# Differential attention with an expert network: the value product of a block as one burst, the second exponentials scaled on GpSimd, the output evicted on VectorE, the out-projection moved up one step

## The chip, the core and the metric

The kernel runs on one core of a Trainium2 chip. The core has TensorE (matrix products, in the profile PE, its weight loads PEld), VectorE (DVE), ScalarE (ACT), GpSimd (POOL) and SyncE (SP), which issues nearly all transfers. The metric is the device time of one execution in microseconds (us); the median of three runs is given.

## What is computed

The reference normalises X (2 x 1024 tokens of 128 values), runs a differential attention with 16 heads on it, and an expert network of a main and two chosen experts per batch, and adds both to X. The attention, cut to what matters:

```python
A1 = jnp.einsum('bhqd,bhkd->bhqk', Q1, K1) * s
A2 = jnp.einsum('bhqd,bhkd->bhqk', Q2, K2) * s
P = jax.nn.softmax(A1, axis=-1) - lam * jax.nn.softmax(A2, axis=-1)
O = jnp.einsum('bhqk,bhkd->bhqd', P, V)
Ocat = jnp.transpose(O, (0, 2, 1, 3)).reshape(O.shape[0], O.shape[2], -1)
Y = Ocat @ Wo + bo
```

All is float32. The kernel writes the two softmaxes with their sums l1 and l2 of exponentials e1 and e2: it builds p = e1 - e2 * (lam * l1 / l2), multiplies by V and Wo, and puts the factor 1 / l1 on at the very end, when the rows are added to Y.

## The kernel before

The attention has 2 batches x 16 heads x 8 query tiles of 128 rows, 256 steps. Each engine has its own program, written out by hand, with counters (semaphores) between them; the order inside an engine is the order of its program. A function `step(g, k)` per engine gives what it does at one step; `attention` writes 16 steps (`BODY`, two heads) out, loops over them, and writes the first and last 16 out apart, with some steps behind the end in which the pipeline drains. Four steps make a block (`QB`), `kb` is the block and `j` the step in it.

One step, for query tile n, in the order in which its data flows:

- TensorE, `scores` (L502): two tiles of 128 x 1024 scores, s = 0 and 1, four instructions each, into one of three PSUM slots of 1024 columns. The slots go round over the score tiles and the projections of the next head.
- VectorE, `row_max` (L861): the maximum of each tile. ScalarE, `exps` (L683): the exponentials, s = 0 to `p_mix`, s = 1 to `e2_buf` (a part of `work`), both four steps deep, with their sums in `l_sum`.
- VectorE, one step later: reciprocals of both sums (L894) into `l_inv`, -lam * l1 (L895) into `l1_neg`, and the scaling of e2 with both factors, one TENSOR_SCALAR of 128 x 1024 (L899). It raises `scaled`.
- GpSimd: the addition e1 + e2 (L412), 128 x 1024, raises `mix_done`. The program of GpSimd also splits the weights of a head to come (`split_w`, L350 to L357, once in 8 steps), in the first steps prepares the expert network (L373 to L399), and in the last head splits its first weights (L426, L429).
- TensorE, `turn`, three steps later (`LAG`): eight transposes of p in two halves of four (L514), each half evicted by ScalarE (`evac_pt`, L696) to `pt`, which holds two blocks.
- TensorE, `pv` (L528): per block eight products of 128 x 64 weights (V) with 512 columns, even ones to the lower and odd ones to the upper 64 rows of the bank `o_ps`. They go in pairs; `PV_AT` puts pair 0 at the first half of step 3, pair 1 at its second half, and pairs 2 and 3 at the two halves of step 0 of the next block.
- ScalarE at step 1 evicts `o_ps` to `o_t` (L703, waits for `pv_done`). TensorE at step 2, first half, does the out-projection of four 128 x 128 products (`out_proj`, L540) into `o_ps` again. VectorE at step 2 adds the four tiles to `y_acc` with the factor 1 / l1 (`add_y`, L873) and raises `y_evac`, on which the next block's first pair waits.

Twice per head TensorE also does a projection of the next head (L458), of which ScalarE makes the high part (L662) and VectorE the low part (L806). Behind the attention comes the expert network (L585, L598, L732 to L738, L438, L958, L964).

On ScalarE the exponential of s = 0 waits until the transposes of the tile four steps back have been made, that of s = 1 until its addition has been made (both buffers are four deep). On TensorE the transposes of step n - 3 wait for `mix_done` and stand between the two score tiles of step n.

## Time and profile before

| | before |
|---|---|
| median of 3 runs | 1380.82 us (1380.06 to 1381.09) |
| profiled execution, whole time | 1380.4 us |
| its span | 1378.6 us |
| TensorE busy | 1292.9 us, 94% |
| VectorE busy | 1173.6 us, 85% |
| ScalarE busy | 1063.3 us, 77% |
| GpSimd busy | 783.6 us, 57% |
| mean granted TensorE clock | 0.99 |

The busy time of an engine counts its compute instructions. Matrix products are pipelined and their ends are modelled, so the shares of TensorE say less than the pitch from one group to the next. The profile's waits say how long an engine stood before a line and whose instruction ended that. An engine that isn't the bottleneck may stand idle at no cost, so the wait that ends last in a stretch is what matters.

### The profile page before, as it was taken

What the parts mean: (1) busy time and instruction counts of PE and PEld (TensorE: products, weight loads), DVE (VectorE), ACT (ScalarE), POOL (GpSimd) and SP (SyncE); (2) the same over time, 40 slices, a digit from 0 to 9 for tenths busy, and PEclk for the clock granted to TensorE, in tenths of its full rate; (3) what the DMA queues carried; (4) which work ended last, traced back from release to release, by engine and by line L of the source; (5) the groups of instructions that cost most, each with busy time, mean ns of one, the idle gap of its engine ahead of it and who ended that gap; (6) DMA issues with size and microseconds to landing.
All of it is one profiled execution on the core that took longest, in us unless ns stands there. A gap on an engine that the chain in (4) does not pass through costs nothing.

```text
span 1378.6 us, 21990 instructions
## 1 busy us (share of the span) xinstructions
PE 1292.9 (94%) x6658; PEld 859.8 (62%) x6658; DVE 1173.6 (85%) x1745; ACT 1063.3 (77%) x1787; POOL 783.6 (57%) x423
## 2 busy tenths in 40 slices
PE   3879999999999999999999999999999999998787
PEld 2646666666666666666666666666666666655576
DVE  7768888888888888888888888888888888886998
ACT  2168888888888888888888888888888888887764
POOL 3078555556555555555555565556555555576765
PEclk9999999999999999999999999999999999999988
DMA  6974444334333444444443343334444444400000
GB/s 146 331 165 103 102 102 102 87 86 92 86 85 87 98 103 103 103 103 102 99 103 89 85 92 87 85 87 95 103 103 103 103 103 99 99 1 1 1 16 16
DMA packets 89822, 129.37 MB, mean 94 GB/s; under 512 B 44484, under 2 KB 62404, under 8 KB 89796
## 3 DMA queue, kind: packets, MB, share of 16 engines
q1 hardware_dynamic: 89092, 128.89, 40.7%
q8 instruction: 14, 0.23, 0.1%
q10 hardware_dynamic: 576, 0.15, 0.1%
q14 instruction: 12, 0.10, 0.0%
q0 software_dynamic: 128, 0.01, 0.0%
HBM read 18.91 MB, written 9.44 MB: 21 GB/s over the span
## 4 chain that ended last, share of the span: by engine, by line
PE 62%; DVE 17%; issue 8%; ACT 5%; POOL 3%; SPq 3%; DMA 1%; DVEq 1%; ACTq 0%; POOLq 0%
PE ps L502 25%; PE ps L528 16%; PE ps L514 12%; PE ps L458 7%; DVE small L861 6%; DVE y_acc L873 3%; ACT pt L696 2%; PE ps L540 2%; DVE pt L964 2%; SPq L251 2%; POOL p_mix L412 2%; ACT p_mix L683 2%; DVE work L958 2%; DVE y_acc L943 1%; DVE work L806 1%
## 5 line engine op out<-in xcount | busy, mean ns | idle before, releaser
L412 POOL TENSOR_TENSOR p_mix<-p_mix,work 128x1024 f32<-128x1024 f32 x256 | 609.3, 2380 | 506.6 <-DVE work L899 506.6
L861 DVE TENSOR_REDUCE small<-ps 128x1 f32<-128x1024 f32 x512 | 619.8, 1220 | 161.6 <-PE ps L502 152.9
L502 PE MATMUL ps<-k_hi,q_st 128*128 128x512 f32 x1024 | 362.6, 435 | 8.1 <-DMA q_st<-work 4.3
L683 ACT ACTIVATE p_mix<-ps,small 128x1024 f32<-128x1024 f32 x256 | 286.8, 1120 | 103.8 <-DVE small L861 103.8
L696 ACT ACTIVATE pt<-ps 128x512 f32<-128x512 f32 x512 | 305.2, 596 | 66.4 <-PE ps L514 61.0
L683 ACT ACTIVATE work<-ps,small 128x1024 f32<-128x1024 f32 x256 | 286.3, 1118 | 70.0 <-DVE small L861 69.7
L514 PE MATMUL ps<-ident,p_mix 128*128 128x128 f32 x2048 | 311.2, 274 | 23.1 <-ACT pt L696 14.6
L502 PE MATMUL ps<-k_lo,q_st 128*128 128x512 f32 x1024 | 320.8, 395 | 0.0
L514 PEld LDWEIGHTS ps<-ident,p_mix 128*128 128x128 f32 x2048 | 241.7, 140 | 123.1 <-issue 38.7
L502 PEld LDWEIGHTS ps<-k_hi,q_st 128*128 128x128 f32 x1024 | 158.7, 189 | 195.9 <-issue 125.8
L528 PE MATMUL ps<-pt,v_h 128*64 128x512 f32 x1024 | 276.6, 619 | 0.0
L899 DVE TENSOR_SCALAR work<-work,small 128x1024 f32<-128x1024 f32 x256 | 227.9, 890 | 9.3
L502 PEld LDWEIGHTS ps<-k_lo,q_st 128*128 128x128 f32 x1024 | 192.4, 188 | 43.8
L438 POOL TENSOR_TENSOR work<-work 128x1024 f32<-128x1024 f32 x24 | 76.0, 3166 | 37.0 <-DVE work L958 37.0
L806 DVE SCALAR_TENSOR_TENSOR work<-ps,small,work 128x1024 fp32r<-128x1024 f32 x64 | 81.6, 1276 | 3.6 <-ACT work L662 3.5
L873 DVE SCALAR_TENSOR_TENSOR y_acc<-ps,small,y_acc 128x128 f32 (+1 forms) x256 | 71.8, 343 | 8.5 <-PE ps L540 7.8
L528 PEld LDWEIGHTS ps<-pt,v_h 128*64 128x64 f32 x1024 | 50.9, 135 | 44.4 <-issue 44.4
L662 ACT ACTIVATE work<-ps,small 128x1024 fp32r<-128x1024 f32 x64 | 71.7, 1120 | 8.2 <-PE ps L458 5.2
L598 PE MATMUL ps<-w,pt 128*128 128x128 f32 x384 | 55.1, 305 | 23.8 <-DVE pt L964 18.8
L598 PEld LDWEIGHTS ps<-w,pt 128*128 128x128 f32 x384 | 51.6, 216 | 31.3 <-DVE pt L964 23.7
L540 PE MATMUL ps<-wo_dup,o_t 128*128 (+1 forms) x512 | 67.7, 275 | 0.2 <-ACT o_t L703 0.2
L540 PEld LDWEIGHTS ps<-wo_dup,o_t 128*128 128x128 f32 x512 | 62.2, 192 | 0.6 <-ACT o_t L703 0.6
(118 smaller groups left out, 910.0 us busy)
## 6 DMA issues: line engine op xcount, KB each, us to landing
k_hi<-work SPq DMA_DIRECT2D x128, 256.0 KB, 4.8
k_lo<-work SPq DMA_DIRECT2D x128, 256.0 KB, 4.8
q_st<-work SPq DMA_DIRECT2D x128, 256.0 KB, 4.4
v_scratch<-pt SPq DMA_DIRECT2D x16, 512.0 KB, 6.4
v_h<-v_scratch SPq DMA_DIRECT2D x32, 256.0 KB, 4.4
wqk_raw<-in_L_attn_Wk SPq DMA_DIRECT2D x31, 64.0 KB, 1.7
wqk_raw<-in_L_attn_Wq SPq DMA_DIRECT2D x31, 64.0 KB, 1.9
x_all<-in_L_attn_X SPq DMA_DIRECT2D x2, 512.0 KB, 5.3
```

The lines of the kernel that those rows point to most:

```text
L412: pool.tensor_tensor(e1, e1, e2, ALU.add).then_inc(mix_done, 1)
L458: mm = pe.matmul(into[:, half * BANK:(half + 1) * BANK], wt[:, w * P:(w + 1) * P], a[:, bass.ds(t0 + half * BANK, BANK)], start=j == 0, st ...
L502: mm = pe.matmul(slot[SLOT[tile]][:, cols], qs4[:, par, s, q0:q0 + P], kk[:, par, s, cols], start=j == 0, stop=j == 1)
L514: mm = pe.transpose(pt_ps[:, c * P:(c + 1) * P], p_mix[:, col:col + P], ident[:, :])
L528: mm = pe.matmul(o_ps[half * D:(half + 1) * D, :], vh4[:, (kb // 2) % 2, c, :], pt4[:, kb % 2, c, :], start=c < 2, stop=c >= KC - 2, skip_ ...
L540: mm = pe.matmul(o_ps[:, t * E:(t + 1) * E], o_t[:, col:col + P], wo_dup[:, bass.ds(head * E, E)], start=True, stop=True, skip_group_check ...
L598: mm = pe.matmul(out_ps, hidden[u % 4][:, t * P:(t + 1) * P], w24[:, 0 if f == 0 else TOPK * b + f, c, :], start=i == 0 and t % 4 == 0, st ...
L683: act.activation((p_mix, e2_buf)[s][:, k % 4 * S:(k % 4 + 1) * S], slot[SLOT[k, s]], ACT.Exp, bias=neg_max[:, m:m + 1], scale=1.0, accum_o ...
L696: act.activation(pt4[:, kb % 2, half * 4:half * 4 + 4, j * P:(j + 1) * P], pt_ps.rearrange("p (c q) -> p c q", c=4), ACT.Copy).then_inc(pt ...
L861: dve.tensor_reduce(neg_max[:, m:m + 1], slot[SLOT[k, s]], AX.X, ALU.max, negate=True)\
L873: add = dve.scalar_tensor_tensor(out=tile, in0=o_ps[:, t * E:(t + 1) * E], scalar=l_inv[:, r1:r1 + 1], in1=tile, op0=ALU.mult, op1=ALU.add)
L899: dve.tensor_scalar(e2, e2, l_inv[:, r + 1:r + 2], l1_neg[:, e:e + 1], ALU.mult, ALU.mult)\
```

## The change

- The four pairs of a block's value product are issued in one piece, at step 3, first half, of the next block.
- The scaling of e2 goes from VectorE to GpSimd, ahead of the addition, as one TENSOR_SCALAR of 128 x 1024 with the same two factors. GpSimd now waits for the reciprocals (`recip_done`), and its addition waits for its own scaling (`scaled`). `l1_neg` becomes four columns deep, and VectorE waits, before it writes it, for the scaling of four steps before.
- The eviction of `o_ps` goes from ScalarE at step 1 to VectorE at step 0, behind the first maximum.
- The out-projection goes from step 2, first half, to step 0, second half, of the block; the sum into `y_acc` goes from step 2 to the end of step 1.
- On VectorE the reciprocals stand ahead of the second maximum of a step.
- GpSimd's steps are written out, with no loop.

```diff
-PV_AT = {(3, 0): 0, (3, 1): 2, (0, 0): 4, (0, 1): 6}
-OUT_AT = (2, 0)
+PV_AT = (3, 0)
+OUT_AT = (0, 1)
...
-        l1_neg = small[:, 172:174]
+        l1_neg = small[:, 172:176]
...
             def step(g, k):
-                n = g * BODY + k
+                n, km = g * BODY + k, (k - 1) % BODY
                 if now(g, k, 1):
-                    e1 = p_mix[:, (k - 1) % 4 * S:((k - 1) % 4 + 1) * S]
-                    e2 = e2_buf[:, (k - 1) % 4 * S:((k - 1) % 4 + 1) * S]
+                    e1 = p_mix[:, km % 4 * S:(km % 4 + 1) * S]
+                    e2 = e2_buf[:, km % 4 * S:(km % 4 + 1) * S]
+                    pool.wait_ge(recip_done, 2 * n)
+                    pool.tensor_scalar(e2, e2, l_inv[:, 2 * km + 1:2 * km + 2], l1_neg[:, km % 4:km % 4 + 1],
+                                       ALU.mult, ALU.mult).then_inc(scaled, 1)
                     pool.wait_ge(scaled, n)
                     pool.tensor_tensor(e1, e1, e2, ALU.add).then_inc(mix_done, 1)
...
-            attention(pool, step, 1)
+            for n in range(STEPS + 1):
+                step(n // BODY, n % BODY)
...
-            def pv(g, kb, c0):
+            def pv(g, kb):
...
-                for c in (c0, c0 + 1):
+                for c in range(KC):
...
-                back = 1 if j == 3 else 2
-                if (j, half) in PV_AT and now(g, k - j, back * QB):
-                    pv(g, kb - back, PV_AT[j, half])
+                if (j, half) == PV_AT and now(g, k - j, QB):
+                    pv(g, kb - 1)
...
-                if j == 1 and now(g, k - j, 2 * QB):
-                    act.wait_ge(pv_done, g * (BODY // QB) + kb - 1)
-                    act.activation(o_t[:, (kb % 2) * BANK:(kb % 2 + 1) * BANK], o_ps, ACT.Copy).then_inc(o_evac, 1)
...
                 if now(g, k):
                     row_max(g, k, 0)
+                if j == 0 and now(g, k - j, 2 * QB):
+                    dve.wait_ge(pv_done, g * (BODY // QB) + kb - 1)
+                    dve.tensor_copy(o_t[:, (kb % 2) * BANK:(kb % 2 + 1) * BANK], o_ps).then_inc(o_evac, 1)
...
-                if j == 2 and now(g, k - j, 2 * QB):
-                    add_y(g, kb)
-                if now(g, k):
-                    row_max(g, k, 1)
                 if now(g, k, 1):
                     dve.wait_ge(exp_done, 2 * m + 2)
+                    after(dve, scaled, m - 3)
                     dve.reciprocal(l_inv[:, r:r + 2], l_sum[:, l:l + 2]).then_inc(recip_done, 1)
                     dve.tensor_scalar(l1_neg[:, e:e + 1], l_sum[:, l:l + 1], lam_neg, None, ALU.mult)\
                         .then_inc(recip_done, 1)
-                    dve.wait_ge(recip_done, 2 * m + 2)
-                    e2 = e2_buf[:, km % 4 * S:(km % 4 + 1) * S]
-                    dve.tensor_scalar(e2, e2, l_inv[:, r + 1:r + 2], l1_neg[:, e:e + 1], ALU.mult, ALU.mult)\
-                        .then_inc(scaled, 1)
+                if now(g, k):
+                    row_max(g, k, 1)
+                if j == 1 and now(g, k - j, 2 * QB):
+                    add_y(g, kb)
```

## Rows read from the trace of the kernel before

**Rows 1.** The page's part 1: busy us, share of the span, instructions.

```profile
PE 1292.9 (94%) x6658; PEld 859.8 (62%) x6658; DVE 1173.6 (85%) x1745; ACT 1063.3 (77%) x1787; POOL 783.6 (57%) x423
```

**Rows 2.** Waits: engine, line, whom it waited for, us in total, times, longest.

```profile
POOL p_mix L412 <- DVE work L899: 506.6, 245, 18.6
```

**Rows 3.** Busy time of one head: PE, PEld, DVE, ACT, POOL, clock, DMA, GB/s.

```profile
680.70:717.70 37.00, 36.47 (x190) 23.74 (x188) 31.83 (x51) 30.51 (x53) 20.72 (x11) 1.00 0.43 95
```

**Rows 4.** The chain in order of time: start us, us it accounts for, what.

```profile
714.27 1.01 PE ps L528 x4
715.28 1.12 PE ps L502 x4
...
722.74 0.89 PE ps L540 x8
...
736.24 0.44 PE ps L514 x4
736.67 0.93 PE ps L502 x4
...
738.04 1.39 PE ps L458 x6
...
1259.74 1.87 PE ps L528 x8
```

**Rows 5.** Groups by form, VectorE and ScalarE: busy us, mean ns, idle before.

```profile
L861 DVE TENSOR_REDUCE small<-ps 128x1 f32<-128x1024 f32 x512 | 619.8, 1220 | 161.6 <-PE ps L502 152.9
L899 DVE TENSOR_SCALAR work<-work,small 128x1024 f32<-128x1024 f32 x256 | 227.9, 890 | 9.3
L806 DVE SCALAR_TENSOR_TENSOR work<-ps,small,work 128x1024 fp32r<-128x1024 f32 x64 | 81.6, 1276 | 3.6 <-ACT work L662 3.5
...
L703 ACT ACTIVATE o_t<-ps 128x512 f32<-128x512 f32 x64 | 37.6, 587 | 0.4 <-PE ps L528 0.4
```

**Rows 6.** GpSimd's groups by form, and line L399 alone (ns min/median/max).

```profile
L381 POOL TENSOR_SCALAR b_bc<-b_bc,small 128x128 f32<-128x128 f32 x5 | 2.9, 604 | 0.0
...
L363 POOL COPY y_acc<-gb_bc 128x2048 f32<-128x2048 f32 x1 | 1.9, 1887 | 0.0
...
L343 POOL CAST k_hi<-w_raw 128x1024 fp32r<-128x1024 f32 x1 | 1.0, 1041 | 5.8 <-DMA w_raw<-in_L_attn_Wv 5.8
...
L399 POOL TENSOR_SCALAR w<-w,small x5: 1560/1692/1952, 113.0 to 133.7; 128x512 f32<-128x512 f32 x5
```

**Rows 7.** Lines L412 and L899 alone: ns min/median/max, first and last start.

```profile
L412 POOL TENSOR_TENSOR p_mix<-p_mix,work x256: 2352/2378/2404, 67.4 to 1253.6; 128x1024 f32<-128x1024 f32 x128
...
L899 DVE TENSOR_SCALAR work<-work,small x256: 811/814/2766, 66.5 to 1250.7; 128x1024 f32<-128x1024 f32 x128
```

**Rows 8.** GpSimd in order of time: start us, us, line, operation, idle before.

```profile
166.61 2.39 POOL L412 TENSOR_TENSOR p_mix<-p_mix,work 128x1024 f32<-128x1024 f32 x1 [1.56 <-DVE work L899]
168.95 0.40 POOL L350 TENSOR_TENSOR wqk_raw<-wqk_raw,small 128x128 f32<-128x128 f32 x1
169.44 0.61 POOL L354 TENSOR_TENSOR wqk_hi<-wqk_raw,small 128x256 fp32r<-128x256 f32 x1
170.13 0.73 POOL L357 TENSOR_TENSOR wqk_lo<-wqk_raw,wqk_hi 128x256 fp32r<-128x256 f32 x1
```

**Rows 9.** Three steps of the last head, and TensorE in them.

```profile
1232.27:1247.59 15.32, 12.96 (x69) 8.77 (x70) 13.02 (x20) 12.14 (x21) 15.08 (x10) 1.00 0.00 0
...
1244.88 0.66 PE L514 MATMUL ps<-ident,p_mix 128*128 128x128 f32 x4 [1.30 <-POOL p_mix L412]
```

**Rows 10.** Busy time where GpSimd prepares the experts, and splits w1.

```profile
91.01:135.20 44.19, 38.41 (x188) 24.98 (x188) 31.46 (x49) 29.85 (x51) 39.57 (x34) 0.92 0.46 98
1224.22:1247.59 23.37, 20.97 (x109) 12.98 (x107) 20.99 (x30) 17.99 (x33) 22.35 (x15) 1.00 0.00 0
```

**Rows 11.** TensorE behind a transfer, and the granted clock of that stretch.

```profile
95.39 1.22 PE L502 MATMUL ps<-k_hi,q_st 128*128 128x512 f32 x2 [4.31 <-DMA q_st<-work]
...
95.00:100.00 5.00, 4.61 (x12) 2.33 (x12) 1.23 (x1) 1.65 (x3) 4.76 (x7) 0.50 0.03 7
```

More of the change, by code:

```diff
@@ L515, in turn @@
                 mm.then_inc(pt_ready, 1)
-            def pv(g, kb, c0):
+            def pv(g, kb):
                 blk = g * (BODY // QB) + kb
-                if c0 == 0:
-                    pe.wait_ge(pt_evac, 2 * QB * (blk + 1))
-                    after(pe, y_evac, blk)
-                    if kb % 2 == 0:
-                        pe.wait_ge(v_loaded[kb // 2], 16 * (g + 1))
-                for c in (c0, c0 + 1):
+                pe.wait_ge(pt_evac, 2 * QB * (blk + 1))
+                after(pe, y_evac, blk)
+                if kb % 2 == 0:
+                    pe.wait_ge(v_loaded[kb // 2], 16 * (g + 1))
+                for c in range(KC):
                     half = c % 2
@@ L530, in pv @@
                                    skip_group_check=True)
-                if c0 == KC - 2:
-                    mm.then_inc(pv_done, 1)
+                mm.then_inc(pv_done, 1)
             def out_proj(g, kb):
@@ L880, in step @@
                 m, km = g * BODY + k - 1, (k - 1) % BODY
-                l, r, e = (km % 4) * 2, km * 2, km % 2
+                l, r, e = (km % 4) * 2, km * 2, km % 4
                 if now(g, k):
                     row_max(g, k, 0)
+                if j == 0 and now(g, k - j, 2 * QB):
+                    dve.wait_ge(pv_done, g * (BODY // QB) + kb - 1)
+                    dve.tensor_copy(o_t[:, (kb % 2) * BANK:(kb % 2 + 1) * BANK], o_ps).then_inc(o_evac, 1)
                 p = k - 1
```

## Prediction, made before the changed kernel was seen or run

> **What bounds the kernel now.** I read the page's first part and the long idle times of the waits first. TensorE is busy for 94% of the span and GpSimd for 57% [rows 1], and GpSimd's idle time is nearly all one wait: before its addition (L412) it stands for 506.6 us in 245 pieces until VectorE's scaling (L899) is done [rows 2]. GpSimd therefore has room now, and it is fed late. The middle of the attention repeats every two blocks, which is one head of 8 query steps. The stretch of one head lasts 37.00 us, with TensorE busy 36.47, VectorE 31.83, ScalarE 30.51 and GpSimd 20.72 [rows 3]. The chain in order of time shows what these 37 us are. Score tiles cost 0.93 us, groups of four transposes 0.44, a projection 1.39, an out-projection 0.89, a pair of the value product 1.01, and the score tile that comes behind a pair costs 1.12 and not 0.93 [rows 4]. Per head that is 16 x 0.93 + 16 x 0.44 + 2 x 1.39 + 2 x 0.89 + 8 x (1.01 + 0.19) = 36.1 us, so TensorE bounds the head and about 0.9 us is left to waits.
>
> **The burst (removes turns of the array).** Today each of the four pairs of a block stands alone between tiles of other shapes: 1.20 us each with the slower score tile behind it. Late in the trace two pairs stand side by side, eight instructions in 1.87 us [rows 4]; the second pair adds 0.86. So a pair inside a burst costs 0.34 less than a lone one; three of four pairs gain: 1.02 us for a block, 65 us for 64 blocks. This is worth its full price only while TensorE is the bound. It also puts 1.01 + 3 x 0.86 = 3.6 us in one piece between two score tiles (step 3 of a block), so the second score tile of that step, its maximum and its exponential come later.
>
> **The eviction and the out-projection.** ScalarE loses one 0.59 us copy a block, VectorE gets one at its step 0 with a wait for the product. Queued behind that wait are the low part, the reciprocal and the second maximum. The product was issued one step earlier on TensorE, so the wait is short. The nearest rows for the copy of 512 columns are ScalarE's own 587 ns and, as the upper end, VectorE's 1220 ns for a maximum over 1024 columns of PSUM [rows 5]. I take 0.7; both ends are hidden, because VectorE gives back far more: the scaling, 890 ns in each of 256 steps [rows 5]. VectorE's load per head goes from 31.8 to about 31.8 - 7.1 + 1.4 = 26.1 us. The out-projection at step 0, second half, now waits on TensorE for VectorE's copy, and the next step's score tiles queue behind it. TensorE reaches it two groups of transposes and a score tile (0.44 + 0.93 + 0.44 = 1.8 us) after the first score tile of the step; VectorE needs the maximum and the copy for that, 1.2 + 0.7 = 1.9 us. I count the 0.1 us at zero, hidden under GpSimd's bound (below); with TensorE as the bound it is 6 us in 64 blocks, and up to 38 if the copy costs its upper end. The sum into y_acc (L873) moves with it, at zero, since VectorE has room.
>
> **The scaling on GpSimd (adds the term that decides).** It costs GpSimd one TENSOR_SCALAR of 128x1024 with two operations and two scalar columns per step, in line ahead of the addition, which also waits for it. The trace of before has no such instruction. The nearest rows are the same opcode with one operation and one scalar column. 128x128 takes 604 ns and 128x512 takes 1560 (shortest) to 1952 ns [rows 6]. From 128 to 512 columns the slope is (1560 - 604) / 384 = 2.49 ns per column, so 1024 columns take 604 + 896 x 2.49 = 2.83 us. I take the shortest of the 512-column rows, since the longer ones may be lengthened by VectorE's work beside them: VectorE's scaling is itself 811 ns at the shortest and 2766 at the longest [rows 7], so the two engines get in each other's way, and that scaling is what the change takes away. With the median of 1692 ns the slope is 2.84 and the price 3.14 us, 79 us more in the sum.
>
> The bounds: below, a one-input copy that runs a column in about 0.83 ns, 1041 ns for 1024 columns; above, the second operation costs one more such pass, (1887 - 1041) / 1024 = 0.83 ns per column or 0.85 us [rows 6], so 3.68 us. I take 2.83, the row of the same opcode. The addition itself is steady, 2378 ns [rows 7], with 2.34 us from its start to the start of a next instruction that waits for nothing; an instruction that waits for the one ahead of it on GpSimd starts 0.08 us after that ends [rows 8]. A step on GpSimd: 2.83 + 0.08 + 2.34 = 5.25 us. The weight split (L350 to L357) takes 1.91 us a head [rows 8]. One head then needs 8 x 5.25 + 1.91 = 43.9 us of GpSimd, against 37.0 that the head takes now and about 35 that TensorE would need. **The bound moves to GpSimd**, and what TensorE, VectorE and ScalarE save becomes waiting.
>
> **A rule of the notes against these rows.** The Trainium skill (GPSIMD Engine Reference, section 4.1, Engine selection) says that one-input elementwise work on GpSimd runs roughly at line rate and only two-input work is about twice as slow as on VectorE. The plain copies fit the rule (1041 ns for 1024 columns), TENSOR_SCALAR does not (1560 ns for 512) [rows 6]. By the rule the step would be 1.04 + 0.08 + 2.34 = 3.46 us and GpSimd would stay under TensorE: that is the first rival below.
>
> **Does GpSimd really get its inputs in time?** TensorE stops at a step until the addition of three steps before is done (L512), with the step's second score tile behind it. Let the addition for step n-3 end at T. In the worst step (step 3 of a block, burst and projection) the second score tile of step n is done at T + 0.66 + 3.6 + 1.12 = T + 5.4, its maximum at about 6.6 (1.22 us), its exponential some 1.2 us later, and the high part on ScalarE (about as long as the exponential) and the low part (1.28) hold VectorE until about 10.3; then comes the reciprocal [rows 5]. GpSimd still has two steps to do meanwhile and asks for it at T + 2 x 5.25 = 10.5. So it is just in time, elsewhere with some 5 us to spare. I add 3 us for the whole kernel (0.1 per head), with 0 to 16 (0.5 per head) as bounds.
>
> That such a regime exists is seen in before: in the last head GpSimd has the w1 splits to do between additions. The stretch of three steps takes 15.32 us, GpSimd busy 15.08 and TensorE 12.96 at full granted clock, and TensorE's transposes wait for the addition, once for 1.30 us [rows 9]. That is 5.11 us a step where 4.63 is usual.
>
> **The sum**, for the profiled execution (span 1378.6, 1.8 around it, 0.4 below the median shown). The first scaling starts at 66.5 [rows 7] and GpSimd can start there. Additions and scalings: 256 x 5.25 = 1344.0. Thirty weight splits: 57.3. What GpSimd does once: the weights of the experts in the first heads, 39.57 us busy in their stretch less seven additions (16.4) and a split (2.1) = 21.0, and the w1 splits, 22.35 less four additions (9.4) = 13.0 [rows 10]. The last addition ends at 66.5 + 1344.0 + 57.3 + 21.0 + 13.0 = 1501.8 instead of 1255.9 [rows 7]. Behind it follow 1378.6 - 1255.9 = 122.7 us of expert network as now. Span 1624.5; with 1.8 and 0.4 it is 1626.7, with the 3 us above **1630 us**, 18% slower.
>
> **The rivals.**
> - *Faster: a long TENSOR_SCALAR is cheap on GpSimd.* Decides from 1.97 us: (37.0 - 1.91) / 8 - 2.42. Below that TensorE keeps the bound and the burst pays: 1380.8 - 65 = 1316 us (1322 with the copy's 0.1 us a block). For it: GpSimd is idle for 506.6 us, the price is extrapolated, copies are that fast. Against: it would need 1024 columns for 0.4 us more than 512 take in the rows. Chance 0.05; 0.01 more for a price just at the point.
> - *The second operation costs a pass of its own:* 3.68 us, 6.10 a step, 1630 + 256 x 0.85 = 1848 us. For it: nothing in the trace shows a two-operation form on GpSimd. Against: the price of the one-operation form (about 3 times a copy's) looks like a loop that holds a place for the second. Chance 0.20, with values between it and the forecast.
> - *TensorE falls to half its clock in its new pauses.* In before it stands 4.31 us for a transfer and is granted 0.50 of its clock just behind [rows 11]. At half clock TensorE's 34 to 35 us of a head become nearly 70, over the 43.9. Against: its new pauses are at most 5.25 us less the 2.7 of two score tiles and two groups of transposes, so 2.5 us, and in the stretch of [rows 9] the clock stays at 1.00. If a tenth of the heads run so: 3.2 x 26 = 83 us more, 1713. Chance 0.06.
> - *The change doesn't do what it says:* the burst gains nothing inside, as its pairs load weights in turn. It would be hidden under GpSimd's bound, so it changes nothing above.
>
> **How the numbers follow.** The forecast (TENSOR_SCALAR at 2.65 to 3.15 us, 1585 to 1710) gets 0.68. The range runs from 1590 to 1855: it takes in the dear second operation and leaves out the cheap rival, the extremes of the clock's, and anything above one extra pass. A measurement of this kernel can tell 0.2% from no change. Faster 0.05, within 0.2% 0.01, slower 0.94.
>
> **What would show it.** Right: GpSimd busy over 95% from 70 to 1500 us; one head every 44 us; TensorE's and its weight loads' waits on L412 in the place of GpSimd's wait on L899; the new TENSOR_SCALAR near 2.8 us; TensorE about 80% busy; a burst of 16 instructions in about 3.6 us with one slow score tile behind. Wrong: a TENSOR_SCALAR below 2 us; GpSimd idle before it with the reciprocal or the exponential as releaser (the ring of three steps then bounds, not GpSimd); granted clock under 1.00 in the middle.

## The result, and the profile after

The changed kernel takes 1408.78 us (median, 1407.42 to 1409.46), the kernel before on the same chip 1380.59 (1380.06 to 1381.09). The ratio is 1.0203, with a 95% interval of 1.0185 to 1.0221: 28 us slower, where 1630 us was forecast with a range from 1590 to 1855. The direction was right and the size wrong by 221 us.

In short: the scaling on GpSimd costs 1.20 us and not 2.83, so GpSimd doesn't bound the middle of the attention. What is lost there is lost behind the burst, which VectorE and ScalarE can't make good between two bursts; at both ends GpSimd does bound.

The page of the changed kernel, part 1 (it answers to [rows 1]), then three of its groups of part 5: busy us, mean ns | idle before, and who ended it.

```profile
PE 1279.2 (91%) x6658; PEld 868.2 (62%) x6658; DVE 991.9 (71%) x1553; ACT 1001.8 (71%) x1723; POOL 1083.9 (77%) x679
...
L858 DVE TENSOR_REDUCE small<-ps 128x1 f32<-128x1024 f32 x512 | 623.8, 1222 | 374.9 <-PE ps L506 369.4
...
L412 POOL TENSOR_SCALAR work<-work,small 128x1024 f32<-128x1024 f32 x256 | 307.1, 1200 | 210.3 <-DVE small L892 208.3
L696 ACT ACTIVATE pt<-ps 128x512 f32<-128x512 f32 x512 | 307.4, 600 | 218.6 <-PE ps L518 215.4
```

The new TENSOR_SCALAR on GpSimd takes 1200 ns, not 2830. GpSimd is busy for 77% of the span and for 80% of a head in the middle (30.27 of 37.66 us, below), not for over 95%, and still stands 208.3 us for the reciprocals (L892). VectorE gave up 181.7 us of work (1173.6 to 991.9) and its maximum now waits 369.4 us for score tiles, where it waited 152.9 [rows 5]. No engine is full over the whole. What the kernel before had as waits of GpSimd is spread over VectorE, ScalarE and GpSimd.

The busy time of one head of the changed kernel in the columns of [rows 3], and of 7.94 us in it in which TensorE isn't on the chain:

```profile
703.16:740.82 37.66, 36.11 (x189) 23.96 (x188) 26.33 (x45) 28.63 (x52) 30.27 (x20) 1.00 0.42 94
732.33:740.27 7.94, 7.18 (x37) 5.00 (x37) 7.55 (x15) 6.69 (x13) 7.52 (x5) 1.00 0.75 165
```

The head takes 37.66 us instead of 37.00. VectorE is busy for 26.33 of it (26.1 was forecast), GpSimd for 30.27. TensorE's own work should have come down to 36.1 - 2.0 = 34.1 us. So some 3.6 us of a head are now lost to waits, where 0.9 were. The busy column (36.11) hides most of them, because the modelled end of a group of products lies up to 0.2 us behind the start of the next. The starts of TensorE's groups in the timeline show them: against the prices of the prediction, the groups of this head are late by 3.6 us in sum, and those of a head of the kernel before (680.7 to 717.7) by 0.9.

Where they are is seen in the chain of the changed kernel, in order of time (start us, us accounted for, what), one head:

```profile
703.23 3.58 PE ps L530 x16
706.81 1.15 PE ps L506 x4
707.98 1.23 DVE small L858
709.24 0.64 ACT work L683
...
710.99 0.66 PE ps L518 x4
...
721.72 3.58 PE ps L530 x16
...
730.36 0.30 DVE o_t L883
...
730.96 1.27 DVE work L803
...
732.42 1.14 DVE small L858
...
736.86 0.86 ACT work L683
...
740.27 0.63 PE ps L518 x4
```

Twice in a head the burst stands as 16 instructions in 3.58 us, with one slow score tile (1.15 us) behind. Behind the first, the chain goes to VectorE and ScalarE for three microseconds (707.98 to 710.99). Behind the second it leaves TensorE at 729.20 and comes back at 740.27: eleven microseconds of one copy, one low part, maxima, exponentials and evictions, back to back. TensorE works beside them for most of that time. By the starts of its groups it loses 2.2 us in this stretch, 0.5 behind the first burst, and 0.9 between 717.8 and 720.1, where the chain goes over a low part. The chain of the kernel before leaves TensorE too, for 3.1 and 6.4 us of a head, with 0.9 us lost. The same place in VectorE's own order of time (start us, us, idle before):

```profile
707.98 2.59 DVE L858 TENSOR_REDUCE small<-ps 128x1 f32<-128x1024 f32 x2 [4.12 <-PE ps L506]
...
726.48 1.23 DVE L858 TENSOR_REDUCE small<-ps 128x1 f32<-128x1024 f32 x1 [3.58 <-PE ps L506]
```

VectorE stands 4.12 and 3.58 us behind a burst with nothing to do, and is then the last of the chain. The two belong together: the idle time is lost and the work comes later in one heap. By the program, the three PSUM slots are what keeps VectorE from having work in stock; no run changed their number, so that part is argued and not shown.

The 28 us by place, from the starts of GpSimd's additions (L412, now L415), eight to a head. The first two heads take 45.94 + 41.33 = 87.3 us where they took 43.26 + 36.13 = 79.4, so 7.9 more; the first addition starts 1.1 earlier and the third head takes 1.1 less; 28 heads at 37.63 in the mean instead of 37.07 give 15.7; the last seven steps take 37.2 us instead of 31.7, 5.5 more; what follows the last addition 1.0. That makes 7.9 - 2.2 + 15.7 + 5.5 + 1.0 = 27.9, the difference of the two spans (1406.5 and 1378.6).

The last seven steps, in which GpSimd also splits the first weights of the experts, in the changed kernel (first line) and in before (second line):

```profile
1243.40:1280.50 37.10, 30.43 (x152) 20.12 (x151) 18.80 (x35) 22.56 (x40) 36.12 (x25) 0.92 0.01 2
...
1221.90:1253.60 31.70, 28.41 (x152) 17.21 (x150) 28.89 (x41) 23.40 (x42) 29.41 (x18) 1.00 0.00 1
```

GpSimd is busy for 36.12 of 37.10 us there, so in these steps it does bound the changed kernel.

### The profile page after: what moved, and what is told of

The parts are those of the page before. It is cut to its first block, busy times and chain, and to the rows that moved or that the text cites. A ratio compares the mean times of both kernels' runs of the same rounds, so it can differ in the third digit from the quotient of the medians.

```text
span 1406.5 us, 21919 instructions
## 1 busy us (share of the span) xinstructions
PE 1279.2 (91%) x6658; PEld 868.2 (62%) x6658; DVE 991.9 (71%) x1553; ACT 1001.8 (71%) x1723; POOL 1083.9 (77%) x679
## 4 chain that ended last, share of the span: by engine, by line
PE 48%; DVE 20%; ACT 14%; issue 10%; POOL 7%; DMA 1%; DVEq 0%; ACTq 0%; POOLq 0%
PE ps L530 16%; PE ps L506 16%; PE ps L518 7%; PE ps L462 6%; DVE work L803 6%; ACT pt L696 5%; DVE small L858 5%; ACT work L683 4%; ACT p_mix L683 4%; POOL p_mix L415 3%; DVE pt L959 2%; PE ps L541 2%; POOL work L412 2%; DVE work L953 1%; DVE y_acc L938 1%
## 5 line engine op out<-in xcount | busy, mean ns | idle before, releaser
L858 DVE TENSOR_REDUCE small<-ps 128x1 f32<-128x1024 f32 x512 | 623.8, 1222 | 374.9 <-PE ps L506 369.4
L415 POOL TENSOR_TENSOR p_mix<-p_mix,work 128x1024 f32<-128x1024 f32 x256 | 610.1, 2383 | 21.3
L412 POOL TENSOR_SCALAR work<-work,small 128x1024 f32<-128x1024 f32 x256 | 307.1, 1200 | 210.3 <-DVE small L892 208.3
L518 PE MATMUL ps<-ident,p_mix 128*128 128x128 f32 x2048 | 320.7, 279 | 51.3 <-ACT pt L696 35.5
L518 PEld LDWEIGHTS ps<-ident,p_mix 128*128 128x128 f32 x2048 | 235.0, 141 | 186.5 <-ACT pt L696 103.9
L530 PE MATMUL ps<-pt,v_h 128*64 128x512 f32 x1024 | 236.4, 604 | 0.0
L506 PEld LDWEIGHTS ps<-k_lo,q_st 128*128 128x128 f32 x1024 | 192.9, 188 | 43.9
L530 PEld LDWEIGHTS ps<-pt,v_h 128*64 128x64 f32 x1024 | 68.3, 138 | 122.8 <-issue 122.8
L598 PE MATMUL ps<-w,pt 128*128 128x128 f32 x384 | 52.1, 294 | 27.0 <-DVE pt L959 22.1
L541 PE MATMUL ps<-wo_dup,o_t 128*128 (+1 forms) x512 | 71.6, 283 | 0.1
L598 PEld LDWEIGHTS ps<-w,pt 128*128 128x128 f32 x384 | 48.8, 206 | 34.1 <-DVE pt L959 25.1
```

The source lines that it names most:

```text
L412: pool.tensor_scalar(e2, e2, l_inv[:, 2 * km + 1:2 * km + 2], l1_neg[:, km % 4:km % 4 + 1], ALU.mult, ALU.mult).then_inc(scaled, 1)
L415: pool.tensor_tensor(e1, e1, e2, ALU.add).then_inc(mix_done, 1)
L506: mm = pe.matmul(slot[SLOT[tile]][:, cols], qs4[:, par, s, q0:q0 + P], kk[:, par, s, cols], start=j == 0, stop=j == 1)
L518: mm = pe.transpose(pt_ps[:, c * P:(c + 1) * P], p_mix[:, col:col + P], ident[:, :])
L530: mm = pe.matmul(o_ps[half * D:(half + 1) * D, :], vh4[:, (kb // 2) % 2, c, :], pt4[:, kb % 2, c, :], start=c < 2, stop=c >= KC - 2, skip_ ...
L541: mm = pe.matmul(o_ps[:, t * E:(t + 1) * E], o_t[:, col:col + P], wo_dup[:, bass.ds(head * E, E)], start=True, stop=True, skip_group_check ...
```

## The experiments

Ratios are to the kernel before on the same chip, with the 95% interval.

**The parts alone.** First the scaling: the kernel before with the scaling on GpSimd.

```diff
+                    pool.wait_ge(recip_done, 2 * n)
+                    pool.tensor_scalar(e2, e2, l_inv[:, 2 * km + 1:2 * km + 2], l1_neg[:, km % 4:km % 4 + 1],
+                                       ALU.mult, ALU.mult).then_inc(scaled, 1)
                     pool.wait_ge(scaled, n)
...
-                    dve.tensor_scalar(e2, e2, l_inv[:, r + 1:r + 2], l1_neg[:, e:e + 1], ALU.mult, ALU.mult)\
-                        .then_inc(scaled, 1)
```

> The kernel before with the scaling of e2 moved to GpSimd alone (written-out steps on GpSimd, l1_neg four deep); lone pairs, eviction on ScalarE and the order on VectorE as before. The changed kernel shows this instruction at 1.20 us, so GpSimd needs about 31 us of a head's 37. Theory A (the burst of 3.6 us in one piece starves VectorE and ScalarE) and theory B (reciprocals ahead of the second maximum) both expect TensorE to stay the bound: head 36.3 to 37.0 us, some 7 us lost in the early stretch where GpSimd prepares the experts, in all 1362 to 1388 us. A rival, that the scaling on GpSimd itself is what cost the 28 us (a later addition), expects 1400 to 1410.

Measured: 1405.92 us, 1.0189 (1.0172 to 1.0206), in the range of the rival and not of the two theories. Second, the kernel before with the burst:

```diff
-PV_AT = {(3, 0): 0, (3, 1): 2, (0, 0): 4, (0, 1): 6}
+PV_AT = {(3, 0): 0}
...
-                for c in (c0, c0 + 1):
+                for c in range(KC):
```

> The kernel before with the eight value products of a block issued in one piece at step 3, first half, and nothing else. Theory A (starving) expects a loss although TensorE saves 2.0 us a head: VectorE still carries the scaling, so 1385 to 1430 us, with VectorE idle some 3.5 us ahead of the first maximum behind each burst. Theory B (order on VectorE) expects the burst to pay in full: 1315 to 1330 us.

Measured: 1430.93 us, 1.0372 (1.0355 to 1.0389), 38.55 us a head. The scaling alone costs 26 us, the burst alone 51, both together with the moves on VectorE 28. So the burst alone is a loss, though it takes 2 us of work from TensorE in each head, and the scaling and the moves, added to it, pay nearly half of that loss back (51 to 28 us).

**The price of the disputed instruction.** In the kernel before, TENSOR_SCALARs of each form ran on a scratch tile on GpSimd, before the attention begins.

```diff
+            for i, (cols, s1, s2) in enumerate(forms * 2):
+                pool.wait_ge(probed, i + 1)
+                v = v_h[:, 0:cols]
+                pool.tensor_scalar(v, v, s1, s2, ALU.mult, *([] if s2 is None else [ALU.mult])).then_inc(probed, 1)
```

> The kernel before with 20 more instructions on GpSimd where it is idle at its start: TENSOR_SCALAR on a tile of its own with 1024, 512 and 128 columns, with one operation and with two, with scalar columns and with immediates, the whole list twice. It measures the price that the forecast got wrong (2.83 us forecast, 1.20 measured, for 1024 columns with two operations). Theory 'form': the one-operation form is the slow one, so 1024 columns take some 2.8 us with one operation and 1.2 with two, and 512 columns 1.5 and 0.7. Theory 'width or tile': the line's other traits (the tile w2, its scalar) make it slow, so one and two operations take the same time at each width, 1.0 to 1.3 us for 1024 columns.

Its line L415 alone, second round: the form of one operation and one scalar column with 1024 columns, and the form of two operations and two scalar columns with 512 (x count: ns min/median/max):

```profile
L415 POOL TENSOR_SCALAR v_h<-v_h,ident x1: 2879/2879/2879, 34.6 to 34.6; 128x1024 f32<-128x1024 f32 x1
...
L415 POOL TENSOR_SCALAR v_h<-v_h,ident x1: 765/765/765, 44.6 to 44.6; 128x512 f32<-128x512 f32 x1
```

With 1024 columns the two-operation form took 1197 and 1201 ns in the two rounds. The one-operation form took 2879 ns in the second round and 3902 ns in the first, where it was the first instruction of its line. In 256 steps of the next run it takes 2838 to 2869 ns, so the extrapolation to 2.83 us was right to 2%, for the other form.

**The rest of the sum, with the price that it was made for.** The changed kernel with the one-operation form (it leaves the factor 1 / l2 out of the computation):

```diff
-                    pool.tensor_scalar(e2, e2, l_inv[:, 2 * km + 1:2 * km + 2], l1_neg[:, km % 4:km % 4 + 1],
-                                       ALU.mult, ALU.mult).then_inc(scaled, 1)
+                    pool.tensor_scalar(e2, e2, l1_neg[:, km % 4:km % 4 + 1], None,
+                                       ALU.mult).then_inc(scaled, 1)
```

> The changed kernel with the one-operation form of the scaling on GpSimd, 2.88 us for 128x1024 by the measured price instead of 1.20. It leaves the factor 1 / l2 out of the computation. It gives the changed kernel the price that the prediction had worked out for it, so it tries all the rest of the prediction's sum. If that sum holds: a step of GpSimd is 2.88 + 0.08 + 2.36 = 5.3 us, a head 8 x 5.3 + 1.9 = 44.4, the median 1650 us (1620 to 1680), GpSimd busy over 93% of the attention, and TensorE waits for the addition in every step. If the steps' latency (the ring of three steps) bounds in place of GpSimd's load, the head is over 45.5 us with GpSimd idle before the scaling, and the median over 1690.

Measured: 1681.03 us (1680.08 to 1683.03), 1.2186 (1.2165 to 1.2206), at the upper end of what was expected. A group of the page of this kernel, and its chain around a burst:

```profile
L412 POOL TENSOR_SCALAR work<-work,small 128x1024 f32<-128x1024 f32 x256 | 728.9, 2847 | 64.9 <-DVE small L892 64.9
```

```profile
724.36 2.83 POOL work L412
727.19 0.07 issue
727.27 2.35 POOL p_mix L415
729.66 0.66 PE ps L518 x4
730.32 5.28 PE ps L530 x16
735.60 1.14 PE ps L506 x4
...
741.25 1.27 DVE work L803
...
742.81 2.86 POOL work L412
```

GpSimd bounds now, as the prediction had it: a step of 5.28 us in the chain. Once a head the chain leaves it, over burst, score tiles, maximum, copy and low part. That is the step that the prediction had followed as the worst, by another path: the prediction went from the second score tile over its maximum, its exponential and the high part to the low part; the chain goes over the projection, the next step's first score tile, the maximum of that and VectorE's copy. With a burst of 3.58 us the reciprocals are done 11.4 us after the addition (776.40 to 787.81), where the prediction had 10.3. GpSimd then stands 2.65 us where the burst took 5.28 us, and 0.95 in the next head, where it took 3.58. The prediction had 0.1 a head, with 0.5 as the bound.

The 5.28 us burst is the prediction's rival of the half clock, to which it gave a chance of 0.06. Two bursts of this kernel, each behind a stop of TensorE of 2.30 us (windows in the columns of [rows 3]; the first is the front part of its burst):

```profile
707.10:710.00 2.90, 2.90 (x9) 0.97 (x10) 0.00 (x0) 1.69 (x3) 2.82 (x3) 0.50 0.09 25
...
776.45:780.68 4.23, 4.23 (x21) 1.54 (x21) 0.00 (x0) 1.69 (x3) 4.15 (x2) 1.00 1.00 227
```

The first was granted 0.50 of the clock, the level of 1.2 GHz, and took 5.18 us; the second was granted 1.00 and took 3.58. What decides between them behind the same stop isn't shown. Of the 64 bursts of this kernel 45 are longer than 3.58 us. In the 28 middle heads the burst that stands behind GpSimd's work is so each time, and costs nothing; the burst on the chain is so in twelve. These twelve heads are 46.8 us long and the other sixteen 45.1. So 12 x 1.7 = 20 us are the clock's, and 28 x (45.08 - 43.9) = 33 are the late turn and a price 0.02 us higher. These 53 us are about the distance from 1630 to 1681.

**Where the first heads lose.** The changed kernel with the scaling on VectorE in the first and last 16 steps (at the hand-over VectorE waits once for an addition):

```diff
+                    if BODY <= n < STEPS - BODY:
                         pool.wait_ge(recip_done, 2 * n)
```

> The changed kernel with the scaling on VectorE in the first 16 and the last 16 steps only, where GpSimd also prepares the experts and splits w1. Reading the pitch of the additions, the first two heads take 7.9 us longer than before and the last 7 steps some 5 us. If that is GpSimd's load: 1394 to 1399 us, the middle unchanged at 37.6 a head. If it is the burst in a not yet filled pipeline: within 3 us of 1408.

Measured: 1405.96 us, 1.0181 (1.0164 to 1.0198), in the range of the rival. The heads tell more than the total. The first head of the changed kernel (first line) and of this one (second line):

```profile
66.34:112.28 45.94, 36.26 (x176) 25.04 (x175) 29.10 (x45) 32.80 (x57) 42.06 (x36) 0.96 0.66 155
...
67.93:109.88 41.95, 33.72 (x172) 22.93 (x171) 34.45 (x52) 31.51 (x56) 34.08 (x29) 1.00 0.60 145
```

In the changed kernel GpSimd is busy for 42.06 of 45.94 us, since it prepares the expert network there [rows 10]. Without the scaling it has 34.08, and the first two heads take 81.0 us instead of 87.3. So GpSimd bounds the changed kernel by its load here, as it does in the last seven steps. Over the whole kernel only 2.8 us are left of these 6.2: this kernel starts its first addition 1.6 us later, the third head takes 1.2 us more, the two heads before the last 0.5 and 1.7, and the last seven steps 1.3 less.

**The moves on VectorE.** The changed kernel with the second maximum ahead of the reciprocals, as in before:

```diff
+                if now(g, k):
+                    row_max(g, k, 1)
                 if now(g, k, 1):
                     dve.wait_ge(exp_done, 2 * m + 2)
```

> The changed kernel with the second maximum of a step ahead of the reciprocals on VectorE again, as before. Theory B expects most of the loss back and the saving of the burst seen: 1335 to 1365 us. Theory A expects little: 1395 to 1412 us.

Measured: 1436.76 us, 1.0416 (1.0399 to 1.0433), slower than either theory expected. And with eviction, out-projection and sum where before has them:

```diff
-OUT_AT = (0, 1)
+OUT_AT = (2, 0)
...
+                if j == 1 and now(g, k - j, 2 * QB):
+                    act.wait_ge(pv_done, g * (BODY // QB) + kb - 1)
+                    act.activation(o_t[:, (kb % 2) * BANK:(kb % 2 + 1) * BANK], o_ps, ACT.Copy).then_inc(o_evac, 1)
```

> The changed kernel with the eviction on ScalarE at step 1, the out-projection at step 2 and the sum at step 2 again, as before; burst, scaling on GpSimd and the order on VectorE stay. Theory 'the eviction on VectorE delays the low part and the reciprocal': 1385 to 1400 us. Theory 'it unloads ScalarE in the ring behind the burst': slower than the changed kernel, 1412 to 1435 us.

Measured: 1423.72 us, 1.0308 (1.0291 to 1.0325). In the changed kernel both moves gain, 28 and 15 us. With the maximum first, the chain goes over GpSimd once a head:

```profile
708.11 0.12 DVE small L894
...
708.32 1.21 POOL work L412
...
709.60 2.38 POOL p_mix L415
711.98 1.19 POOL work L412
...
713.24 2.38 POOL p_mix L415
...
715.67 0.66 PE ps L518 x4
```

The reciprocals stand behind a maximum of 1.2 us, and TensorE's transposes wait for two full steps of GpSimd behind them.

**Is it the length of the burst?** The changed kernel with the burst in two halves, at both halves of step 3:

```diff
-PV_AT = (3, 0)
+PV_AT = {(3, 0): 0, (3, 1): 4}
```

> The changed kernel with the burst cut into two pieces of two pairs, at the first and at the second half of step 3. It gives up one lone-pair turn, 0.34 us a block or 22 us of TensorE time. Theory A expects that VectorE and ScalarE no longer run dry: 1345 to 1380 us. Theory B expects no gain: 1405 to 1430 us.

Measured: 1428.89 us, 1.0354 (1.0336 to 1.0371). With four lone pairs where before has them, the eviction on VectorE at step 1 and out-projection and sum at step 2:

```diff
-PV_AT = (3, 0)
-OUT_AT = (0, 1)
+PV_AT = {(3, 0): 0, (3, 1): 2, (0, 0): 4, (0, 1): 6}
+OUT_AT = (2, 0)
```

> The changed kernel with the value product in four lone pairs at their old places (hence the eviction at step 1, the out-projection at step 2 and the sum at step 2); scaling on GpSimd, eviction on VectorE and reciprocals ahead of the second maximum stay. Theory 'uneven load' (between bursts TensorE has only 2.7 us of work in a step, less than the 3.1 to 3.3 us that ScalarE and VectorE need, and three PSUM slots can't carry work over a burst): with the product spread, the head falls to 36.3 to 37.2 us, 1370 to 1392 us in all, faster than the changed kernel although TensorE has 2 us a head more to do. Rival 'the burst pays and the scaling on GpSimd takes all': slower than 1408, 1430 to 1475 us.

Measured: 1402.15 us, 1.0156 (1.0139 to 1.0173). And the projections out of the steps of the burst, in the changed kernel:

```diff
-PROJ_AT = (1, 3)
+PROJ_AT = (0, 2)
```

> The changed kernel with the two projections of a head at steps 0 and 2 and not 1 and 3, so that none stands in the step of a burst and its low part can be made while TensorE is in the burst. Theory 'ring behind the burst' (the burst and the projection of step 3 leave VectorE a queue of copy, low part, reciprocal and maxima, 11 us of the chain per head without TensorE): 1.5 to 2.5 us a head back, 1330 to 1365 us. Rival 'GpSimd's additions come too late by their own load': within 8 us of the changed kernel's 1408.

Measured: 1419.12 us, 1.0281 (1.0264 to 1.0298). Lone pairs cost TensorE 2 us more a head, and yet the kernel is 6.6 us faster with them. Two halves are slower than one burst, by 20 us, which my account didn't expect. The product is then ready later for VectorE's copy. The trace of that run fits this: the weight loads of the out-projection wait for the copy for 11.7 us and its products for 6.8 (5.9 and none in the changed kernel), and once a head both stand on its chain; that this makes the 20 us isn't shown. That the projection in the step of the burst does harm is refuted: moved out of it, the kernel is 10 us slower.

**Is it uneven load?** If VectorE and ScalarE can't catch up between bursts, lighter ones must make the burst pay. First ScalarE alone, in the changed kernel and in before; it evicts two of four transposed tiles, so the other two are left out of the product:

```diff
-                act.activation(pt4[:, kb % 2, half * 4:half * 4 + 4, j * P:(j + 1) * P],
-                               pt_ps.rearrange("p (c q) -> p c q", c=4), ACT.Copy)
+                act.activation(pt4[:, kb % 2, half * 4:half * 4 + 2, j * P:(j + 1) * P],
+                               pt_ps.rearrange("p (c q) -> p c q", c=4)[:, 0:2, :], ACT.Copy)
```

> The changed kernel in which ScalarE evicts only two of the four transposed tiles of a half (256 of 512 columns), so the other half of pt stays as it was and that part of the product is left out of the computation. It takes some 0.2 us off each of two evictions a step. Theory 'uneven load': ScalarE is on the chain in the steps between bursts, so 6 of 8 steps get up to 0.4 us shorter: 1.2 to 2.6 us a head, 1325 to 1370 us. Rival 'GpSimd's lateness sets the pitch': 1398 to 1408.

> The same lighter eviction in the kernel before. TensorE bounds it (36.1 of 37.1 us a head), so both theories expect little: at most 0.9 us a head, 1352 to 1380 us. If it gains as much as the changed kernel does, ScalarE's latency and not the uneven load is what the pair of runs shows.

Measured: 1401.29 us, 1.0151 (1.0134 to 1.0168), and 1366.49 us, 0.9901 (0.9884 to 0.9917). The kernel before gains more (14 us) than the changed one (7.5), so ScalarE alone isn't it. Then both engines, with maxima over the first 512 of 1024 columns:

```diff
-                dve.tensor_reduce(neg_max[:, m:m + 1], slot[SLOT[k, s]], AX.X, ALU.max, negate=True)
+                dve.tensor_reduce(neg_max[:, m:m + 1], slot[SLOT[k, s]][:, 0:BANK], AX.X, ALU.max, negate=True)
```

> after_light_act with VectorE lightened too: each maximum is taken over the first 512 of 1024 columns only (the maximum of the other half is left out, as is half of the eviction to pt), 0.5 us less for each of two maxima a step. Theory 'uneven load' (between bursts VectorE and ScalarE together can't keep up with TensorE): now the burst's saving is seen, head 34.5 to 35.8 us, 1310 to 1350 us, and at least 15 us faster than before_light_both. Rival 'GpSimd's row of scaling and addition sets the pitch': 37 us a head, 1385 to 1400.

> The same two cuts in the kernel before. TensorE's own work of 36.1 us a head is the floor: 36.1 to 36.6 us a head, 1345 to 1366 us. The uneven-load theory expects it to lie above after_light_both, the reverse of the full kernels.

Measured: 1350.31 us, 0.9786 (0.977 to 0.9802), and 1347.16 us, 0.9763 (0.9745 to 0.978). The changed kernel was expected to be at least 15 us faster than before, and is 3 us slower, but its middle is now the faster one: a head takes 35.73 us in the changed kernel and 36.01 in before. Before is bound by TensorE alone; one head of its windows, and below it the chain of the changed one:

```profile
700.00:736.01 36.01, 36.01 (x190) 24.09 (x189) 23.30 (x50) 26.99 (x54) 21.05 (x11) 1.00 0.44 98
```

```profile
736.31 1.23 POOL work L412
...
737.61 2.40 POOL p_mix L415
740.02 1.20 POOL work L412
...
741.29 2.39 POOL p_mix L415
...
743.72 0.65 PE ps L518 x4
744.38 3.58 PE ps L530 x16
```

TensorE's work of a head is 36.01 us, as the prediction had added it up (36.1). In the changed kernel, two steps of GpSimd stand before one burst of each head. So the last run takes GpSimd's scaling out of this comparison: the light kernel before with the burst alone.

```diff
-PV_AT = {(3, 0): 0, (3, 1): 2, (0, 0): 4, (0, 1): 6}
+PV_AT = {(3, 0): 0}
```

> The kernel before with the burst alone, and with the lighter ScalarE and VectorE (two of four transposed tiles evicted, maxima over 512 columns; this part of the computation is left out, as in the pair before). The scaling stays on VectorE, so GpSimd isn't on the chain as it was in the changed kernel with lighter engines. Its partner without the burst is TensorE-bound at a head of 36.01 us and 1347.2 us. If the burst's 2 us a head are hidden only because VectorE and ScalarE can't catch up between bursts, the head is 34.1 to 34.8 and the median 1270 to 1305. If the burst has a cost of its own with TensorE (the stretch of 3.6 us starves the ring of four steps whatever the other engines' load), the head stays at 35.7 to 36.5 and the median at 1340 to 1370.

Measured: 1331.68 us (1329.97 to 1333.48), 0.9649 (0.9633 to 0.9665), a head of 35.40 us, between the two expectations. With light engines the same edit that costs 51 us in the kernel before gains 15.5. That shows that the load of VectorE and ScalarE decides the sign. But only 0.6 of the 2.04 us a head come through. Waits of this kernel from 600 to 900 us, some 8.5 heads (engine, line, whom it waited for: us, times, longest):

```profile
DVE small L860 <- PE ps L502: 94.2, 60, 3.9
ACT pt L695 <- PE ps L514: 63.8, 43, 3.1
...
PEld ps L514 <- ACT pt L695: 10.2, 21, 0.7
```

VectorE still stands up to 3.9 us behind a burst, and TensorE's weight loads wait for evictions in pieces of up to 0.7 us. By the starts of TensorE's groups the remaining 1.4 us of a head are pieces of 0.1 to 0.5 us, from 4 to 9 us behind the end of a burst. So a part of the burst's loss stays even with light engines; whether the slots or the order of the programs set it is open.

**Is it GpSimd's lateness?** In the kernel before with the scaling on GpSimd, the chain once a head:

```profile
735.09 1.21 POOL work L413
...
736.37 2.40 POOL p_mix L416
738.77 0.37 POOL wqk_raw L350
...
739.27 0.62 POOL wqk_hi L354
...
739.96 0.73 POOL wqk_lo L357
740.69 1.20 POOL work L413
...
741.97 2.39 POOL p_mix L416
...
744.49 0.65 PE ps L519 x4
```

The weight split (1.9 us) stands between two additions that TensorE waits for. Moved to other steps, in this kernel to 4 and to 7, and to 7 in the kernel with lone pairs (the edit to 7):

```diff
-SPLIT_W_AT = 5
+SPLIT_W_AT = 7
```

> scale_only with GpSimd's weight split one step earlier (step 4 of the head, where GpSimd stands waiting, and not step 5, where it has three scalings and additions to do in a row). Theory 'GpSimd's additions come too late behind the split': the 0.4 us a head that scale_only lost in the middle come back, 1390 to 1397 us. Rival 'the later addition costs in every step by its latency': within 4 us of scale_only's 1405.9.

> scale_only with the weight split at step 7 and not 5 (at 4 it cost 31 us more). If the lateness of GpSimd behind the split is what scale_only lost in the middle: 37.45 falls to 36.9 to 37.2 us a head, 1388 to 1400 us. If the steps' own latency is: within 4 us of 1405.9.

> lone_pairs with the split at step 7. GpSimd is not on lone_pairs' chain in the middle, so the GpSimd theory expects at most 0.2 us a head, 1395 to 1403 us; as a candidate for a version that beats both it needs under 1380, which would take a head under 36.8.

Measured: 1437.31 us, 1.0412 (1.0394 to 1.0429); 1391.15 us, 1.0078 (1.0061 to 1.0095); 1398.39 us, 1.0132 (1.0115 to 1.0149). Step 4, expected to gain 9 to 16 us, costs 31: its chain still has the split between two additions. At step 7 the head takes 37.06 us, that of before (37.07), and of the 26 us of the scaling 11 remain, 6.6 in the first two heads (45.65 + 40.32 against 79.4) and 5.5 in the last seven steps, less about 1 elsewhere. So in the middle it was one badly placed split that made GpSimd late, not its load. VectorE's 7 us of relief a head then bring nothing, since TensorE bounds. With lone pairs and the changed order on VectorE the head stays at 37.43. The chain of that run has, once a head, VectorE's copy and the reciprocals ahead of the second maximum, which scale_split_7's has not; no run separates the two.

No version tried beats the kernel before with its whole computation.

## Why the prediction was wrong, point by point

**The failed step is the price of the scaling on GpSimd.** It was 1.20 us (1186 to 1220 ns) in place of 2.83. The slope from [rows 6] was sound for the form that it came from; the error was to count the opcode as the nearest row. One operation with a scalar column takes 2879 ns for 1024 columns, two operations with two columns 1198: the form with less to compute is the slower. The argument against the cheap price ("1024 columns for 0.4 us more than 512 take") and the reasoning for the dear one ("a loop that holds a place for the second") both treated the two forms as one. The lower bound of 1041 ns, the plain copy, was the close one, and the stated range left it out. By (2.83 - 1.20) x 256 = 417 us the term was too large.

The Trainium skill (GPSIMD Engine Reference, section 4.1, Engine selection) says that one-input elementwise work on GpSimd runs roughly at line rate. The two-operation form agrees (1198 ns, near the plain copy's 1041), the one-operation form does not (2847 ns in 256 instructions of after_one_op). The prediction had found the disagreement in the rows and extended it to a form that they didn't have.

**That the bound moves to GpSimd** fell with the price: a step is 1.20 + 0.08 + 2.36 = 3.64 us, a head 8 x 3.64 + 1.9 = 31 of 37.7. With 2.85 us it does move, and the sum's 1630 stands against 1681 measured, 3% more. Two small terms were too small: the late turn of the burst (0.1 us a head; about 1), and the half clock (left out of the sum; 20 us). That the forecast came as near as 221 us is luck: at the true price a middle head is set by TensorE and the engines behind it, for which the sum had no term.

**The rival that came true failed too.** Its condition (below 1.97 us) was met, and it promised 1316 us, since TensorE would keep the bound and the burst pay in full. It was 93 us off. The burst does what was said of it: 3.58 us for 16 instructions, one slow score tile, 2 us of TensorE's work a head. But the step that TensorE bounds, so that its saving is the head's, took the mean over a head (36.1 of 37.0) for the state in each step. With the work in one lump, VectorE stands for 3.6 and 4.1 us behind it and ScalarE for up to 3.3, and they have their work then in a heap, at a pitch that TensorE no longer sets. The prediction had seen that "the second score tile, its maximum and its exponential come later", and had costed it only for GpSimd.

**Eviction and out-projection.** The copy takes 681 ns (0.7 was taken), TensorE's weight loads wait for it 5.9 us in 31 pieces (6 was named for a TensorE bound). That VectorE has room was right on the mean and wrong behind the second burst, where the copy (730.36) and the low part stand on the chain. Still, undoing the move costs 15 us.

**The start.** That GpSimd prepares the experts beside the first heads had its own term (21.0 us). At the real price it remains true, and so does the term of the last head (13.0 us): GpSimd's load bounds at both ends of the attention. The first two heads hold 7.9 of the 28 us, of which 6.2 come back there without the scaling, and the last seven steps 5.5.

**The order of reciprocals and maximum**, which the sum held at nothing, is worth 28 us in the changed kernel. With lone pairs, order and eviction together gain 4 us with the split at step 5 (lone_pairs against scale_only) and cost 7 with it at step 7 (lone_split_7 against scale_split_7), so it is not a price that holds without the burst.

## What to carry to other kernels

Price an instruction by a row of its very form, with its number of operations and the kind of its operands; two forms of one opcode differed by 2.4 times here, and not in the direction that the count of operations suggests. Where there is no such row, the range must reach the cheapest one-input row. A saving on an engine that is busy for 97% of a period was lost here because its followers could not catch up behind the lump: before work is gathered into a burst, add up what the next engines must then do between bursts, in order of time and not in the mean. When an engine gets a second job, look for the step in which its other jobs stand before an addition that someone waits for, not at its busy share: moving one split of 1.9 us a head was worth 15 us here.

## What the runs showed of the hardware

- On GpSimd, a multiplication by two scalar columns (two operations) takes 1198 ns for 128x1024 and 765 for 128x512, that by one column 2879 and 1567 (second round of price_forms; the 256 steps of after_one_op have 2847 in the mean). With constants in place of columns it is 1058 and 1136 ns for two operations and 2771 and 2774 for one, in two rounds each, all with 1024 columns.
- A burst of 16 instructions, products with 128x64 weights, takes 3.58 us at a granted clock of 1.00 and 5.18 and 5.28 us with a part of it at 0.50, the level of 1.2 GHz, behind stops of 2.30 and 2.23 us. Of two stops of 2.30 us, one was followed by the lower level and one not.
- A group of four products with 128x64 weights alone between tiles of 128x128 costs 1.01 us, and the score tile behind it 1.12 to 1.15 instead of 0.93; in the burst of 16 such a group costs 0.86 to 0.90.
